# Two chained cross-attentions on one core: x, context and weights handed in transposed as well, instead of being turned on TensorE

## The reference, cut to what matters

```python
# layer 0 (softmax over the 512 queries, axis 1), residual and layer norm
q = emb @ Wq + bq; k = ctx @ Wk + bk; v = ctx @ Wv + bv
w = softmax(q @ k.T / 16, axis=1)          # (512, 1601) per batch
x = layernorm(w @ v + emb) * gamma + beta
# layer 1 (softmax over the 1601 keys, axis -1), output projection and residual
Q = x @ Wq + bq; K = ctx @ Wk + bk; V = ctx @ Wv + bv
out = x + (softmax(Q @ K.T / 16, axis=-1) @ V) @ Wo + bo
```

## Time and profile before

| | us |
|---|---|
| median of 3 runs | 467.43 (467.13 to 467.44) |
| the profiled execution's own time | 466.4 |
| its span, first to last instruction | 464.6 |
| PE / ACT / DVE / POOL busy | 443.7 / 383.7 / 366.8 / 365.0 |

### The profile page before, as it was taken

The page is one execution under the profiler, slowest core; times in us unless marked ns, Lnnn a source line. Parts: engine busy times, 40 slices in busy tenths (PEclk is TensorE's granted clock), DMA queues, the critical chain, the costliest instruction groups (busy, mean ns, idle before and its releaser), DMA issues.

```text
span 464.6 us, 7967 instructions
## 1 busy us (share of the span) xinstructions
PE 443.7 (96%) x2433; PEld 371.6 (80%) x2433; DVE 366.8 (79%) x898; ACT 383.7 (83%) x819; POOL 365.0 (79%) x321
## 2 busy tenths in 40 slices
PE   8798899999999999999999999999999999799796
PEld 8686667887888888888888878888888878687596
DVE  3798978788886988778787888779877887578774
ACT  4899889987999789987899879987899879872473
POOL 0567699979999799887999789987999699963400
PEclk9999999999999999999999999999999999999999
DMA  9400200021100210020200210001100010000001
GB/s 262 130 24 24 71 24 2 23 72 34 36 23 1 72 47 23 24 55 18 70 23 1 71 49 23 24 18 55 46 1 0 3 46 1 0 0 25 23 1 45
DMA packets 23896, 17.29 MB, mean 37 GB/s; under 512 B 1055, under 2 KB 23854, under 8 KB 23854
## 3 DMA queue, kind: packets, MB, share of 16 engines
q1 hardware_dynamic: 23706, 16.66, 11.8%
...
## 4 chain that ended last, share of the span: by engine, by line
PE 79%; ACT 8%; DVE 5%; POOL 4%; issue 4%; DVEq 0%; POOLq 0%; ACTq 0%
PE ps_l L654 11%; PE ps_l L655 10%; PE ps_l L656 9%; PE ps_s L800 9%; PE ps_s L654 8%; PE ps_s L656 8%; PE ps_s L655 8%; ACT p L1048 3%; PE ps_s L774 3%; PE ps_s L841 3%; DVE max L1257 2%; POOL wsum L1376 2%; PE ps_l L687 2%; ACT p L1001 2%; PE ps_s L768 2%
## 5 line engine op out<-in xcount | busy, mean ns | idle before, releaser
L1376 POOL TENSOR_TENSOR wsum<-wsum,p 128x512 f32<-128x512 f32 (+1 forms) x88 | 116.3, 1322 | 13.4 <-ACT p L1007 11.8
L1383 POOL TENSOR_TENSOR p_lo<-p,p_hi 128x512 fp32r<-128x512 f32 (+1 forms) x91 | 117.2, 1295 | 2.6 <-ACT p_hi L1015 2.4
L1001 ACT ACTIVATE p<-s_sb,min 128x512 f32<-128x512 f32 (+1 forms) x104 | 75.4, 726 | 7.5 <-DVE min L1171 5.3
L1171 DVE CUSTOM_DVE_ANT_0 s_sb<-ps_l,cb 128x512 f32<-128x512 f32 (+1 forms) x104 | 70.4, 685 | 13.3 <-ACT p L1001 5.5
L1007 ACT ACTIVATE p<-p,r 128x512 f32<-128x512 f32 (+1 forms) x104 | 74.9, 728 | 1.4 <-DVE r L1178 1.3
L1192 DVE TENSOR_TENSOR p1T_lo<-ps_s,p1T_hi 128x512 fp32r<-128x512 f32 (+1 forms) x91 | 60.6, 683 | 14.4 <-ACT p1T_hi L1056 13.9
L1257 DVE TENSOR_REDUCE max<-ps_s 128x1 f32<-128x804 f32 x58 | 57.1, 992 | 10.0 <-PE ps_s L656 8.6
L1056 ACT CAST p1T_hi<-ps_s 128x512 fp32r<-128x512 f32 (+1 forms) x91 | 52.0, 586 | 14.9 <-PE ps_s L800 12.1
L1015 ACT CAST p_hi<-p 128x512 fp32r<-128x512 f32 (+1 forms) x104 | 63.5, 624 | 0.5 <-PE ps_l L656 0.4
L1048 ACT ACTIVATE p<-ps_s,bias 128x1206 f32<-128x1206 f32 (+1 forms) x58 | 53.6, 927 | 3.6 <-DVE bias L1268 3.1
L800 PE MATMUL ps_s<-ident,p 128*128 128x128 f32 (+1 forms) x364 | 49.6, 273 | 1.5 <-ACT p L1048 1.5
...
## 6 DMA issues: line engine op xcount, KB each, us to landing
...
x_sb<-in_x_dram SPq DMA_DIRECT2D x8, 512.0 KB, 3.6
...
```

The source lines that it names most:

```text
L1001: nc.scalar.activation(p0[0:m, ring0(i), :], s0_sb[0:m, (a + i) % 2, :], ACT.Exp, bias=min0[0:m, i:i + 1], scale=-1.0, accum_out=sum0[0:m, ...
L1171: nc.vector.tensor_tensor_reduce(out=s0_sb[0:m, (a + i) % 2, :], in0=ps_s0[0:m, (a + i) % 2, :], in1=cb[a % 2][0:m, :], scale=-SCALE, scal ...
L1376: nc.gpsimd.tensor_tensor(total, total, p0[0:m, ring0(i), :], ALU.add).then_inc(wsum_done, 1)
L1383: nc.gpsimd.tensor_tensor(p0_lo[0:m, h, :], p0[0:m, ring0(i), :], p0_hi[0:m, h, :].bitcast(F32), ALU.subtract).then_inc(p0_lo_done, 1)
```

## The change

`kernel()` passes transposed copies of x, the context, Wq, Wk and Wv of layer 1 as further inputs, and the bias vectors as ready columns. So:

- PE loses all of `turn_x`, `turn_ctx`, `turn_wq`, `turn_wk` and `turn_vectors`; the bias matmuls read a column broadcast (`weigh_bias`), and DVE's `repeat` goes.
- `xT_sb` and `ctxT_sb` are loaded by DMA. `x_high`, `ctx_high` (ACT) and `xT_low`, `ctxT_low` (DVE) read them from SBUF where they read PSUM before.
- To make room `ctx_sb` has one buffer, and `xT_sb` and `ctxT_sb` one each. `x_sb` keeps two.
- The SP loop loads xT, x, ctxT and ctx of batch c, and then stores batch c-2.
- In batch 0 the four casts of the context move from ACT to POOL (`ctx_split_first`), and the casts `p0_hi` of the six odd tiles move from ACT to DVE (`p0_high_first`).
- All tables are written anew.

```diff
-        wq_sb = [early(EC * E).rearrange("p (c h) -> p c h", c=EC) for _ in range(2)]
+        wqT = [early(EC * E).rearrange("p (h e) -> p h e", h=EC) for _ in range(2)]
...
         x_sb = [sb(f"x_sb{p}", [P, TB, E]) for p in range(2)]
-        ctx_sb = [sb(f"ctx_sb{p}", [P, MT, L]) for p in range(2)]
+        xT_sb = sb("xT_sb", [P, EC, T])
+        ctx_sb = sb("ctx_sb", [P, MT, L])
+        ctxT_sb = sb("ctxT_sb", [P, M])
...
+            def load_xT(c):
+                if c >= 1:
+                    sp.wait_ge(xT_lo_done, EC * c)
+                sp.dma_start(xT_sb[:], xT[bass.ds(c, 1)].rearrange("o (c p) t -> p (o c) t", p=P)).then_inc(xT_loaded, 16)
+
+            def load_ctxT(c, g):
+                if c >= 1:
+                    sp.wait_ge(ctxT_lo_done, GROUPS * (c - 1) + g + 1)
...
             def load_ctx(c, g):
-                if c >= 2:
-                    sp.wait_ge(ctx_lo_done, GROUPS * (c - 2) + g + 1)
-                    sp.wait_ge(pv0_ps, MT * (c - 2) + group(g)[-1] + 1)
+                if c >= 1:
+                    sp.wait_ge(ctx_lo_done, GROUPS * (c - 1) + g + 1)
...
-            for c in range(2, B + 3):
+            for c in range(2, B + 2):
                 if c < B:
+                    load_xT(c)
+                    load_x(c)
+                    for g in range(GROUPS):
+                        load_ctxT(c, g)
                     for g in range(GROUPS):
                         load_ctx(c, g)
-                    load_x(c)
-                if c >= 3:
-                    store(c - 3)
+                store(c - 2)
...
-            def turn_ctx(a, g):
...
-            def turn_x(a, c):
...
+            def weigh_bias(ps, col, w):
+
+                for h in range(EC):
+                    mm = nc.tensor.matmul(ps, col[:, h:h + 1].broadcast_to([P, P]), w[:, h, :], start=(h == 0), stop=(h == EC - 1))
+                return mm
...
-                nc.scalar.copy(ctxT_hi[a % 2][:, lo:hi], ctx_bank(a, g)[:, 0:hi - lo]).then_inc(ctxT_hi_done, 1)
+                nc.scalar.copy(ctxT_hi[a % 2][:, lo:hi], ctxT_sb[:, lo:hi]).then_inc(ctxT_hi_done, 1)
...
-                nc.scalar.copy(xT_hi[:, c, :], x_bank(a, c)[:]).then_inc(xT_done, 1)
+                nc.scalar.copy(xT_hi[:, c, :], xT_sb[:, c, :]).then_inc(xT_done, 1)
...
-                nc.vector.tensor_tensor(ctxT_lo[a % 2][:, lo:hi], ctx_bank(a, g)[:, 0:hi - lo],
+                nc.vector.tensor_tensor(ctxT_lo[a % 2][:, lo:hi], ctxT_sb[:, lo:hi],
                                         ctxT_hi[a % 2][:, lo:hi].bitcast(F32), ALU.subtract).then_inc(ctxT_lo_done, 1)
...
-                nc.vector.tensor_tensor(xT_lo[:, c, :], x_bank(a, c)[:], xT_hi[:, c, :].bitcast(F32), ALU.subtract
+                nc.vector.tensor_tensor(xT_lo[:, c, :], xT_sb[:, c, :], xT_hi[:, c, :].bitcast(F32), ALU.subtract
...
+            def p0_high_first(a, i):
+
+                dve.wait_ge(norm0_done, i + 1)
+                if (held := split_before(a, i)) is not None:
+                    dve.wait_ge(pv0_ps, held)
+                m = rows(i)
+                nc.vector.tensor_copy(p0_hi[0:m, i % RH, :], p0[0:m, ring0(i), :]).then_inc(p0_hi_odd, 1)
...
+            def ctx_split_first(a, g):
+
+                pool.wait_ge(ctx_loaded[g], 16)
+                m = rows(group(g)[0])
+                tiles = slice(group(g)[0], group(g)[-1] + 1)
+                nc.gpsimd.tensor_copy(ctx_hi[0][0:m, tiles, :], ctx_sb[0:m, tiles, :]).then_inc(ctx_hi_first, 1)
...
 GPSIMD_STEADY = (
-    ("rsqrt_var", "b", 0), ("p0_low", "a", 1), ("sum_weights", "a", 2), ("rsqrt_var", "b", 1), ("weigh_u1", "b", 0),
+    ("p0_low", "a", 4), ("p0_low", "a", 5), ("sum_weights", "a", 4), ("sum_weights", "a", 5), ("sum_weights", "a", 6),
...
+        x=inputs["x"], xT=np.asarray(inputs["x"]).transpose(0, 2, 1),
+        ctx=inputs["ctx_512"], ctxT=np.asarray(inputs["ctx_512"]).transpose(0, 2, 1),
```

More of the change, by code:

```diff
@@ L900, in make_w1 @@
+                    pe.wait_ge(cols_loaded[1], 16)
+                    pe.wait_ge(weights_lo_done, 1)
                     make_a(1, s1_bank(2))
-                    pe.wait_ge(reps_done, 2 * EC)
-                    for h in range(EC):
-                        mm = nc.tensor.matmul(s1_bank(2)[:, E:2 * E], bk_rep[1][:, h, :], wqT[1][:, h, :],
-                                              start=(h == 0), stop=(h == EC - 1))
-                    mm.then_inc(made_ps, 1)
+                    weigh_bias(s1_bank(2)[:, E:2 * E], bk_col[1], wqT[1]).then_inc(made_ps, 1)
@@ L906, in make_w1 @@
                 elif i == 1:
[L907 removed]
+                    pe.wait_ge(wv_loaded, 16 * 2)
                     for h in range(EC):
                         nc.tensor.matmul(s1_bank(3)[:, 0:E], wvT[:, h, :], wo_sb[:, h, :], start=(h == 0), stop=(h == EC - 1))
[L910 to L912 removed]
@@ L913, in make_w1 @@
-                    mm.then_inc(made_ps, 1)
-                else:
-                    for h in range(EC):
-                        nc.tensor.matmul(s1_bank(0)[:, 1:2], bk_rep[1][:, h, :], bq_col[1][:, h:h + 1],
-                                         start=(h == 0), stop=(h == EC - 1))
+                    weigh_bias(s1_bank(3)[:, E:2 * E], bv1_col, wo_sb).then_inc(made_ps, 1)
+                else:
+                    pe.wait_ge(u0_done, 1)
+                    weigh_bias(s1_bank(0)[:, 1:2], bk_col[1], cols[1][:, :, 0:1])
@@ L1446 @@
     arrays, args = {}, []
-    for name in _INS:
-        a = np.ascontiguousarray(inputs[name])
+    for name, a in laid_out(inputs).items():
         arrays[f"in_{name}_dram"] = a
```

352 lines of the change are left out of this document (141 added, 211 removed), and 451 rows, old and new, of tables (GPSIMD_HEAD, GPSIMD_STEADY, SCALAR_HEAD, SCALAR_STEADY).

## The result

The kernel got slower, not faster: the changed kernel takes 478.53 us (median of 4 runs, 477.69 to 480.9) against 467.44 (467.13 to 468.44) beside it, a ratio of 1.0251 (95% interval 1.0229 to 1.0273). In a second series it was 1.0201 (1.0175 to 1.0227). The prediction of 456.2 us, with a range of 447.5 to 463, was wrong in sign.

What follows compares the result with a forecast made beforehand. It took PE to bound the six batch periods and ACT the filling part. Gains of 9.6 (periods), 1.5 (filling part with start) and 0.1 us made 11.2: 466.4 to 455.2, plus 1.0 for the median, 456.2 us; range 447.5 to 463.

Steps and rivals of the forecast that it cites:

- The turning: PE's transposes of x and context in each batch: removing them saves 2.3 us, from a 52.4 us period to 50.1.
- nothing on PE replaces them: Claim that the new PE order has as many groups of the other transposes as before, so the 2.3 us stay saved.
- The collisions: DVE's low-part subtractions with two SBUF inputs take turns with POOL: 2.1 us more POOL work a batch, 49.7 in all.
- a fifth: Share of POOL's 5.4 us idle time at the seam between batches taken as kept: 1.1 us, period 50.8.
- The rest of the filling part: From 15.35 to 48.8 us: DVE takes over from ACT as bound, 0.6 us gain, bounds -2 and +4.
- The p-casts: Batch 0's six casts of p moved to DVE: some 0.6 us each, 3.6 us more DVE work.
- Start: Before the first `max0`: without PE's transposes it starts at about 14.5 instead of 15.35 us, 0.9 us gain (0 to 3).
- DMA: Loads of 1.3 MB more per batch into single buffers: no cost taken, up to 1 us a batch as bound.
- Behind 363.2: The part of the kernel after 363.2 us: only one transpose goes, 0.1 us gain.
- The slower rival: Batch seam: POOL's 5.4 us wait all stays, plus 2.1 us collisions: period 55.1, 16 us slower, 483 us; chance 0.05.
- POOL waits of 3 us or more a period: Sign in the batch periods, named beforehand, that would show the forecast wrong in the bad sense.

Runs made afterwards that it cites:

- f1: The kernel before, with every PE transpose of x and of the context issued twice (21 more a batch): 483.4 us, ratio 1.0343.
- e1: The changed kernel, with the low parts of xT and ctxT made from one SBUF input (they hold the whole value): 473.1 us, ratio 1.0137.
- h3: g2 with the low parts of xT and ctxT made from one SBUF input (they hold the whole value): 466.3 us, ratio 0.9986.
- g2: g1 with 21 unused filler matmuls added at six waits of PE in the filling part: 474.3 us, ratio 1.0162.
- f2: The kernel before, with xT_low and ctxT_low taking their first operand from SBUF instead of PSUM (other values): 483.0 us, ratio 1.0333.
- the repeat: The changed kernel profiled and timed again, unedited: 476.7 us, ratio 1.0201.
- g1: The changed kernel, with POOL's multiplication of batch 1's x by u0 moved ahead of the sums of weights: 477.4 us, ratio 1.0219.
- h4: e1 with 12 of PE's transposes in a batch issued twice: 479.2 us, ratio 1.0257.

## Why the prediction was wrong

- **The turning, 2.3 us a batch, period allowed by PE 50.1.** The price was nearly right (f1: 2.0 us). The base was wrong: 53.25 and not 52.4, in five periods and not six. And "nothing on PE replaces them" failed: 1.05 us of it came back, most of it, as I read the rows, as waits for `scores1`'s banks, so the period without collisions is 52.3 (e1, h3).
- **The collisions, "0.4 us of POOL for each of the five long subtractions and 0.1 us for the short one", and "a fifth" of POOL's idle time kept.** The means of the long ones and POOL's 49.7 us of work came out. The step that failed is the fifth. I let POOL keep 1.1 of its 5.4 us of waits and got 50.8. It kept 4.1 in the batch shown (49.55 + 4.1 = 53.7) and 3.6 of 5.5 us of idle time in the mean of the five (49.7 + 3.6 = 53.3). My reason for the fifth, other POOL work between the links of the chain, did not make the waits go. Beside this the collisions delay the very instruction that PE waits for, which I had at nothing: 1.7 us in the short one, 1.2 in one ahead of `scores0`, up to 4.1 at a time, of which PE waits 2.4 us in five periods. Taking the second SBUF input away gives 4.9 us over five inner periods at the least and 8 over the whole kernel (g2 against h3); putting it into the kernel before costs 16 (f2). Why POOL keeps so much of its waits no run shows.
- **"The rest of the filling part", "0.6 us of gain (bounds -2 and +4)".** 6.7 us lost by the first mark (5.8 in the repeat), and 3.75 more in the period behind it, which I had counted as a full period with the gain of the others. I added up work for each engine, took DVE's 35 us as the bound, and got its work nearly right (35.58 us in the new, longer stretch). But no engine's work was the bound. DVE's delays made PE idle, and the clock did the rest: a factor that I had left out altogether, worth 3.1 us in g2 over g1 and, with the early step, 6.8 in h3 over e1. Where the 2.9 us come from that h3 still loses by batch 1 stays open.
- **The p-casts** were dearer in my estimate (0.6 us) than alone (0.41), but one of six took 1.49 beside POOL. The page "VectorE: DVE Perf Modes" of the Trainium skill, section "Mode 2×_2P", has such a copy at two elements a cycle; the 0.41 us, against 0.68 for a subtraction of the same size, agree.
- **Start, 0.9 us:** 0.5 came (14.86). **DMA, nothing:** behind the first cast of xT and the first cast of the context on POOL (which waits until 9.27 us) I saw no engine wait for a new load. **Behind 363.2, 0.1 us of gain:** 1.5 lost, 2.1 in the last period less 0.6 behind it, nearly alike in all variants of the changed kernel (h4 loses 0.9 more).
- **The slower rival**, 483 us, was nearest, and by its mechanism in the inner periods: POOL's work grew, most of its waits stayed, POOL took PE's place on the chain. Its condition, an idle time of POOL of 2.7 us or more, was met, and so was the sign "POOL waits of 3 us or more a period". I gave it 0.05. Its size was wrong: the inner periods stayed at 53.3 and did not reach 55.1, and its 16 us were to come from there; the 11 were lost by the mark of batch 1 and in the last period, for which it had nothing. That the totals lie near each other is luck. Nothing in my list had the clock in it. The sentence on what would make the prediction fall ("the p-casts or the collisions hold up `max0`, so that the first 48.8 us grow") met the filling part.

Left open: a version that computes all and has no two-input subtraction was not built. For instance, one that lets ACT write the high part a second time, into PSUM, so that DVE has one SBUF input, was not tried. Of the versions that compute all, none beats the kernel before.
